# b1 as two rows, a new order of work on all engines, joined y chains and five quantisations on GpSimd in an adaptive-norm FFN kernel

## The chip, the core and the metric

One core of a Trainium2 chip. The metric is device microseconds of one execution. Five engines run their own instruction lists and wait for one another by semaphores: TensorE (PE), VectorE (DVE), ScalarE (ACT), GpSimd (POOL), SyncE (SP, which here only issues DMAs).

## What is computed

x is (2, 1024, 256): two samples of 1024 tokens. Cut to what matters:

```
dg, db, ug, ub = cond @ down_gamma, cond @ down_beta, cond @ up_gamma, cond @ up_beta
down = relu(x @ (down_project * dg + db))               # 256 -> 64, per sample
y    = down @ (up_project * ug + ub) + x                # 64 -> 256
bitlinear(v, w, b) = quant8(rmsnorm(v)) @ ternary(w).T + b
out  = x + bitlinear(gelu(bitlinear(y, w1, b1)), w2, b2)   # 256 -> 1024 -> 256
```

quant8 scales each token by 127 over its largest magnitude, rounds, and divides again. ternary rounds a weight over the mean of all |w| to -1, 0 or 1 and multiplies by that mean. gelu is the exact one.

## The kernel before

The tokens are cut into 8 pairs (k or j, PAIRS) of two slots (s, one for each sample) of 128 tokens. Each engine has its instruction order written out by hand; a helper is called once for each pair or pair and slot, such as `gelu(4, 1)`.

Prologue: `down_weights` and `up_weights` build the conditioned weights (TensorE products, lines 225 to 237, then VectorE, lines 559 to 575). w1 and w2 come by DMA; `absolute_sum` (ScalarE one half, VectorE the other, lines 440 and 577), `weight_sum` (TensorE) and `weight_scale` give the scale, `round_weights`, `lower_weights` and `upper_weights` the ternary weights in fp16. `column_sums` (line 265) adds up w1's columns for the offset that the quantised y carries, `sum_w2` the same for w2.

For each pair: `x_tokens` and `up` (lines 282 to 303) put y for 2 x 128 tokens into PSUM; `largest_y`, `step_y` (VectorE), `square_y`, `quantise_y` (ScalarE, fp16 with an offset). GpSimd's `chain_y(k)` and `inverse_y(k)` (lines 785 to 821) work out the dequantising factor `ydeq` and the inverse with which the bias row is multiplied, nine small instructions for each pair, one waiting for the other; the inverse stands as bf16 pieces beside the quantised y. Pair 0 has `chain_first` instead. `turn_q1(k)` turns this by a DMA transpose on SyncE; pair 0 is turned by TensorE (`transpose_q1`, ScalarE's `copy_q1t`). `first_layer(j, s)` does 4 products of 512 columns with w1 and two with the bias (lines 325 and 333) into PSUM. `gelu(j, s)` writes g, a ring of 4 pairs. `square_g` (line 481, ScalarE) and `largest_g` (line 633, VectorE) read it; `step_g`, then `quantise_g` (line 654) writes fp16 q2. `turn_q2` turns that by DMA for pairs 0 to 5; pairs 6 and 7 go over TensorE (`transpose_q2`) and ScalarE (`copy_q2t`, line 487). `second_layer` (lines 358 and 360), then VectorE's `combine` (line 661) multiplies by `gdeq` (GpSimd's `chain_g`) and adds x, to which GpSimd's `add_b2` (line 852) has added b2. SyncE stores.

b1 is added inside the first layer as bf16 pieces: b1f has nine rows of b1 in each group of 32 partitions, brought by four ScalarE DMAs behind the one of `pk` and behind a memset. GpSimd's `split_b1` (lines 855 to 864) turns them into high, middle and low parts with two passes of a TENSOR_SCALAR and a TENSOR_TENSOR. `keep_warm(n)` is n products of zeros. Nothing else orders the engines than these lists and the semaphores; SyncE's queue is in order too, so a `turn_q2` that waits holds up the turns and stores behind it.

Of the kernel before, what the change touches and what calls it, by code (L numbers as in the profile page):

```python
# [4 lines left out]
P = 128  # L5
SLOTS = 2
# [11 lines left out]
LAST = PAIRS - 1  # L18
ROW = 2 * D + P
# [3 lines left out]
def adaln_ffn(nc, x_tok, x_dim, down_pack, first_pack, w1_t, w2_t, b1_rows, b2_rows, out):  # L23
# [3 lines left out]
    with ExitStack() as ctx:  # L27
# [23 lines left out]
        w2s = sb("w2s", [P, D], F16)  # L51
        b1f = sb("b1f", [P, HALF])
# [16 lines left out]
        neg_half = sb("neg_half", [P, SLOTS])  # L69
# [29 lines left out]
        dpk_in, pk_in, b2_in, b1_zero, b1_in = sem("dpk_in"), sem("pk_in"), sem("b2_in"), sem("b1_zero"), sem("b1_in")  # L99
# [15 lines left out]
        b1_rest, b1_upper, first_done = sem("b1_rest"), sem("b1_upper"), sem("first_done")  # L115
# [9 lines left out]
        q2_ready = sem("q2_ready")  # L125
# [21 lines left out]

        block = ctx.enter_context(nc.Block())

        @block.sync  # L150
        def _(sp):
# [15 lines left out]
            def turn_q1(k):  # L167
                sp.wait_ge(q1_ready, k + 1)
                sp.wait_ge(inv_ready, k + 1)
                sp.dma_start_transpose(q1t[:, k], q1[:, k, :]).then_inc(q1t_in[k - 1], 16)  # L170

            def turn_q2(j, s):
                sp.wait_ge(q2_ready, SLOTS * j + s + 1)
# [20 lines left out]
            turn_q2(1, 0)  # L194
            turn_q2(1, 1)
            turn_q2(2, 0)
            store(0)
            turn_q1(5)
            turn_q2(2, 1)
            turn_q1(6)  # L200
            store(1)
            turn_q2(3, 0)
            turn_q2(3, 1)
            turn_q1(7)
            turn_q2(4, 0)
            turn_q2(4, 1)
            turn_q2(5, 0)
            store(2)
# [10 lines left out]
        def _(pe):  # L219
# [5 lines left out]
            def down_weights():  # L225
# [4 lines left out]
                mm.then_inc(dcond_done, 1)  # L230

# [105 lines left out]
            def transpose_q2(j, s):  # L337

                pe.wait_ge(q2_ready, SLOTS * j + s + 1)
# [44 lines left out]
            first_layer(0, 1)  # L384
            x_tokens(3)
            up(3)
            down(3)
            first_layer(1, 0)
            first_layer(1, 1)
            x_tokens(4)  # L390
            up(4)
            first_layer(2, 0)
            sum_w2()
            first_layer(2, 1)
            x_tokens(5)
            up(5)
            first_layer(3, 0)
            second_layer(0, 0)
            first_layer(3, 1)
            x_tokens(6)  # L400
            up(6)
            first_layer(4, 0)
            second_layer(0, 1)
            second_layer(1, 0)
            first_layer(4, 1)
            x_tokens(7)
            up(7)
            second_layer(1, 1)
            second_layer(2, 0)
            first_layer(5, 0)  # L410
            first_layer(5, 1)
            second_layer(2, 1)
# [3 lines left out]
            first_layer(7, 0)  # L416
            second_layer(3, 1)
            second_layer(4, 0)
            first_layer(7, 1)
            second_layer(4, 1)  # L420
            second_layer(5, 0)
            transpose_q2(6, 0)
            second_layer(5, 1)
            transpose_q2(6, 1)
            transpose_q2(7, 0)
            second_layer(6, 0)
# [6 lines left out]
        def _(a):  # L433
# [38 lines left out]
            def gelu(j, s):  # L472
                a.wait_ge(ffn1_done, SLOTS * j + s + 1)
                if s == 0:
                    a.wait_ge(ydeq_done, j + 1)
# [29 lines left out]
            copy_q1t()  # L505
            round_weights(1)
            square_y(2)
            gelu(0, 0)
            quantise_y(2)
            gelu(0, 1)  # L510
            square_g(0, 0)
            relu(3)
            square_y(3)
            quantise_y(3)
            gelu(1, 0)
            gelu(1, 1)
            square_y(4)
            gelu(2, 0)
            quantise_y(4)
            square_g(0, 1)  # L520
            gelu(2, 1)
            square_y(5)
            quantise_y(5)
            gelu(3, 0)
            square_g(1, 0)
            gelu(3, 1)
            square_g(1, 1)
            square_y(6)
            gelu(4, 0)
            quantise_y(6)  # L530
            square_g(2, 0)
            gelu(4, 1)
            square_g(2, 1)
            square_y(7)
            square_g(3, 0)
            gelu(5, 0)
            quantise_y(7)
            gelu(5, 1)
            square_g(3, 1)
            square_g(4, 0)  # L540
            gelu(6, 0)
            square_g(4, 1)
            square_g(5, 0)
            gelu(6, 1)
# [13 lines left out]
        def _(v):  # L558
# [60 lines left out]

            def largest_y(k):  # L620
# [44 lines left out]
            v.memset(b1f[:], 0.0).then_inc(b1_zero, 1)  # L665
# [6 lines left out]
            down_weights()  # L672
            up_weights()
# [13 lines left out]
            largest_y(2)  # L687
            round_weights(1)
            step_y(2)
            lower_weights(1, 1)  # L690
            add_column_sums()
            upper_weights(1, 1)
            lower_weights(1, 0)
            largest_g(0, 0)
            largest_y(3)
            largest_g(0, 1)
            step_y(3)
# [253 lines left out]
```

## Time and profile before

| | us |
|---|---|
| runs | 75.25, 78.56, 77.22 (median 77.22) |
| the profiled execution | 75.27 |
| its span, first to last instruction | 73.5 |
| mean granted TensorE clock | 0.973 |

The trace's times are of that one execution, counted from the start of its span. "Idle before" names what ended an engine's wait. Start to start of two instructions of one engine is a little less than the duration shown, as the ends overlap.

### The profile page before, as it was taken

Reading aid. Unit: us, or ns where it says so; the run is one execution under the profiler, and the core shown is the slowest. Engines: PE = TensorE matmul, PEld = TensorE weight load, DVE = VectorE, ACT = ScalarE, POOL = GpSimd, SP = SyncE. Lnnn points to the kernel's source line nnn. Section 1 sums busy time; section 2 is a strip of 40 time slices with the busy share of each in tenths; the row PEclk is TensorE's granted clock in tenths of the full one; section 3 lists DMA queues with packets and bytes.
Section 4 is the critical chain, followed back from the end, with each engine's and each line's share of the span. In section 5 each row is a group of like instructions: output and inputs, shape, how many; then the busy total and the mean of one; then the engine's idle time right before and its main releaser. Section 6 shows DMA issues by size and latency. Waiting matters only on the chain.

```text
span 73.5 us, 1375 instructions
## 1 busy us (share of the span) xinstructions
PE 63.8 (87%) x412; PEld 34.9 (47%) x412; DVE 58.1 (79%) x126; ACT 55.1 (75%) x113; POOL 56.5 (77%) x134
## 2 busy tenths in 40 slices
PE   3449995798999999999999999998969998699950
PEld 1042534442733422554355574834416757598830
DVE  4104357998199999799999999999999699999550
ACT  0060157994499949889999999999999999995300
POOL 6700098998889896888879899888899999899700
PEclk9999999955999999999999999999999999999998
DMA  0899999999904004436737709797997996530352
GB/s 6 263 351 288 379 406 430 419 406 428 406 40 92 16 0 89 90 58 123 133 65 143 143 15 270 147 89 167 222 198 145 181 271 118 167 143 16 144 205 73
DMA packets 20478, 13.49 MB, mean 184 GB/s; under 512 B 17748, under 2 KB 18260, under 8 KB 20088
## 3 DMA queue, kind: packets, MB, share of 16 engines
q1 hardware_dynamic: 20256, 12.69, 64.2%
q10 hardware_dynamic: 216, 0.73, 2.9%
q8 instruction: 3, 0.05, 0.3%
q14 instruction: 3, 0.02, 0.1%
HBM read 7.02 MB, written 2.10 MB: 124 GB/s over the span
## 4 chain that ended last, share of the span: by engine, by line
PE 51%; POOL 12%; ACT 11%; DMA 8%; DVE 7%; issue 5%; ACTq 2%; DVEq 0%; POOLq 0%
PE h L325 14%; PE ob L360 12%; DMA b1f<-b_rows 8%; ACT junk_g L481 6%; PE up_ps L302 5%; PE h L333 5%; PE up_ps L293 5%; ACT g L476 5%; POOL b1f L864 3%; DVE q L654 3%; PE ob L252 3%; PE ob L358 2%; POOL b_high L861 2%; PE up_ps L344 2%; ACTq L493 2%
## 5 line engine op out<-in xcount | busy, mean ns | idle before, releaser
L633 DVE TENSOR_REDUCE gtop<-g 128x1 f32<-128x1024 f32 x16 | 19.2, 1207 | 0.7 <-ACT g L476 0.7
L476 ACT ACTIVATE g<-h,ydeq 128x1024 f32<-128x1024 f32 x16 | 17.8, 1127 | 0.2
L481 ACT ACTIVATE junk_g<-g 128x1024 bf16<-128x1024 f32 x16 | 17.1, 1081 | 0.0
L325 PE MATMUL h<-w1q,q1t 128*128 128x512 f16 x64 | 16.5, 380 | 0.0
L360 PE MATMUL ob<-w2q,q2t 128*128 128x256 f16 x128 | 16.3, 272 | 0.0
L360 PEld LDWEIGHTS ob<-w2q,q2t 128*128 128x128 f16 x128 | 12.5, 98 | 1.4
L654 DVE TENSOR_SCALAR q<-g,gm 128x1024 f16<-128x1024 f32 x16 | 11.8, 750 | 0.1
L852 POOL TENSOR_TENSOR x<-x,b 128x512 f32<-128x512 f32 x8 | 10.1, 1271 | 0.0
L325 PEld LDWEIGHTS h<-w1q,q1t 128*128 128x128 f16 x64 | 5.6, 97 | 7.0 <-issue 2.8
L661 DVE SCALAR_TENSOR_TENSOR x<-ob,gdeq,x 128x256 f32<-128x256 f32 x16 | 7.5, 478 | 1.4 <-PE ob L360 1.4
L462 ACT ACTIVATE q<-up_ps,ym 128x256 f16<-128x256 f32 x16 | 6.8, 481 | 0.4 <-DVE ym L629 0.4
L455 ACT ACTIVATE junk_y<-up_ps 128x256 bf16<-128x256 f32 x16 | 6.0, 389 | 1.3 <-DVE ytop L622 1.1
L622 DVE TENSOR_REDUCE ytop<-up_ps 128x2 f32<-128x512 f32 x8 | 5.5, 686 | 1.7 <-PE up_ps L302 1.7
L792 POOL TENSOR_TENSOR yrms<-yvar,neg_half 128x2 f32<-128x2 f32 x7 | 6.1, 873 | 0.6
L358 PE MATMUL ob<-w2s,neg_offset 128*128 128x256 f16 x16 | 4.4, 275 | 2.0 <-DVE x L661 1.7
L861 POOL TENSOR_SCALAR b_high<-b1f,part 128x512 f32<-128x512 bf16 x2 | 1.4, 691 | 5.9 <-DMA b1f<-b_rows 5.8
L830 POOL TENSOR_TENSOR grms<-gvar,neg_half 128x2 f32<-128x2 f32 x7 | 5.5, 780 | 0.6
L302 PE MATMUL up_ps<-wu,act 64*128 64x256 f32 x32 | 5.6, 427 | 0.1
L333 PE MATMUL h<-b1s,q1t 32*128 32x512 bf16 x28 | 5.5, 393 | 0.0
L223 PE MATMUL h<-warm 128*128 128x512 f16 x11 | 4.4, 520 | 1.2 <-DVE warm L664 1.2
L293 PE MATMUL up_ps<-ident,xd 128*128 128x128 f32 x28 | 4.5, 283 | 0.6 <-issue 0.5
L252 PE MATMUL ob<-xd,wd 128*64 128x128 f32 (+2 forms) x24 | 4.6, 513 | 0.0
(104 smaller groups left out, 102.6 us busy)
## 6 DMA issues: line engine op xcount, KB each, us to landing
w<-w_t SPq DMA_DIRECT2D x4, 512.0 KB, 7.7
x<-x_tok SPq DMA_DIRECT2D x2, 1024.0 KB, 13.1
out<-x SPq DMA_DIRECT2D x7, 256.0 KB, 2.3
xd<-x_dim SPq DMA_DIRECT2D x1, 1024.0 KB, 13.0
pk<-first_pack ACTq DMA_DIRECT2D x1, 640.0 KB, 4.2
xd<-x_dim SPq DMA_DIRECT2D x1, 512.0 KB, 9.5
xd<-x_dim SPq DMA_DIRECT2D x1, 256.0 KB, 7.6
out<-x SPq DMA_DIRECT2D x2, 128.0 KB, 1.7
```

The costliest lines, as they stand in the source:

```text
L252: mm = pe.matmul(down_ps[n][H * s:H * (s + 1), :], wd[:, s, c, :], moving, start=(c == 0), stop=(c == DK - 1))
L293: pe.matmul(up_ps[:, s, P * c:P * (c + 1)], x_dims(k)[:, c, s, :], ident32[:, :], start=(c == 0), stop=False, is_transpose=True)
L302: mm = pe.matmul(up_ps[:, s, 0:D], act[rows, k, :], wu[rows, :], start=False, stop=True)
L325: pe.matmul(h_ps[s][:, cols], q1t[:, j, s * DK + c, :], w1q[:, c, cols], start=(i == 0), stop=False)
L333: mm = pe.matmul(h_ps[s][:, HALF * n:HALF * (n + 1)], q1t[rows, j, SLOTS * DK, :].bitcast(BF16), upper_half(bias[rows, :]), start=False, s ...
L360: mm = pe.matmul(out_ps[s], q2t[:, j % RING, s, c, :], w2q[:, c, :], start=False, stop=(c == FK - 1))
L476: a.activation(g[:, j % RING, s, :], h_ps[s][:, :], ACT.Gelu, scale=ydeq[:, j, s:s + 1])\
L481: a.activation(junk_g[:, j % 3, s, :], g[:, j % RING, s, :], ACT.Square, scale=F ** -0.5, accum_out=gmean[:, j, s:s + 1]).then_inc(gsq_don ...
L633: v.tensor_reduce(gtop[:, j, s:s + 1], g[:, j % RING, s, :], AX.X, ALU.max, apply_absolute_value=True)\
L654: v.tensor_scalar(q2[:, j % RING, s, :], g[:, j % RING, s, :], gm[:, j, s:s + 1], OFFSET, ALU.mult, ALU.add).then_inc(q2_ready, 1)
L661: v.scalar_tensor_tensor(x[:, j, s, :], out_ps[s], gdeq[:, j, s:s + 1], x[:, j, s, :], ALU.mult, ALU.add).then_inc(out_ready, 1)
L852: p.tensor_tensor(x[:, j], x[:, j], b2[:, :].unsqueeze(1).broadcast_to([P, SLOTS, D]), ALU.add)\
```

## The change

- b1 comes as one DMA of 2 rows of 512 (ScalarE's queue, no wait); TensorE's `spread_rows` multiplies it by a 2 x 128 pattern of ones, made by GpSimd, so that PSUM has b1's half in nine rows of each group of 32; `split_b1` moves to VectorE, between `down_weights` and `up_weights`, and reads PSUM in its first pass. The memset of b1f goes.
- `pk` is loaded by SyncE right behind `dpk`.
- `keep_warm`: 17 products where there were 11, one fewer ahead of `up_weights`.
- `chain_y` and `inverse_y` run over (0), (1), (2, 3), (4, 5), (6, 7): five chains, not eight. `turn_q1`, and `gelu` of slot 0, wait for the chain that holds their pair.
- `quantise_g` of slot 1 of pairs 1 to 5 is GpSimd's, with a semaphore of its own; `gelu` now also waits, from pair 4 on, for the square and the quantisation of the pair that had its place in the ring.
- The hand-written orders of all engines change: on TensorE `column_sums` ahead of `first_layer(0, 0)`, `weight_sum(1)` after `up(2)`; on VectorE `absolute_sum(1)` after the rounding of w1; on ScalarE the y work ahead of the gelus and `gelu(7, 1)` ahead of `square_g(6, 0)`; SyncE's queue and GpSimd's `add_b2`s are spread anew.

```diff
+CHAINS = [(0, 1), (1, 2), (2, 4), (4, 6), (6, 8)]
+BY_POOL = [(1, 1), (2, 1), (3, 1), (4, 1), (5, 1)]
             sp.dma_start(dpk[:], down_pack).then_inc(dpk_in, 16)
+            sp.dma_start(pk[:], first_pack).then_inc(pk_in, 16)
...
+            def spread_rows():
+                pe.wait_ge(spread_set, 2)
+                pe.wait_ge(b1_in, 16)
+                pe.matmul(ob[:, 0, :], spread_b1[:, :], b1[:, :], start=True, stop=True).then_inc(b1_spread, 1)
...
             down_weights()
-            keep_warm(2)
+            spread_rows()
+            keep_warm(1)
             up_weights()
             down(0)
             x_tokens(0)
+            keep_warm(1)
             up(0)
             keep_warm(3)
             down(1)
+            keep_warm(2)
             weight_sum(0)
+            keep_warm(3)
             x_tokens(1)
             up(1)
             keep_warm(3)
             down(2)
+            keep_warm(1)
             transpose_q1()
             x_tokens(2)
+            up(2)
             weight_sum(1)
-            up(2)
+            column_sums()
             first_layer(0, 0)
-            column_sums()
...
-            a.dma_start(pk[:], first_pack).then_inc(pk_in, 16)
-            a.wait_ge(b1_zero, 1)
-            for r in range(4):
-                a.dma_start(b1f[32 * r + 1:32 * r + 10, :], b1_rows[r % 2]).then_inc(b1_in, 16)
+            a.dma_start(b1[:], b1_rows).then_inc(b1_in, 16)
...
             gelu(7, 0)
             square_g(5, 1)
+            gelu(7, 1)
             square_g(6, 0)
+            copy_q2t(6, 0)
             square_g(6, 1)
+            copy_q2t(6, 1)
             square_g(7, 0)
-            gelu(7, 1)
-            copy_q2t(6, 0)
+            copy_q2t(7, 0)
             square_g(7, 1)
-            copy_q2t(6, 1)
-            copy_q2t(7, 0)
             copy_q2t(7, 1)
...
+            def split_b1():
+                v.wait_ge(b1_spread, 1)
+                v.wait_ge(part_set, 5)
+                for n, rows in enumerate((ob[:, 0, :], b1f[:, :])):
+                    if n:
+                        v.wait_ge(b1_rest, n)
+                    v.tensor_scalar(b1_high[:, :], upper_half(rows), part[:, n:n + 1], 0.0, ALU.mult, ALU.add)\
+                        .then_inc(b1_upper, 1)
+                    v.wait_ge(b1_upper, n + 1)
+                    v.tensor_tensor(b1f[:, :], rows, b1_high[:, :], ALU.add).then_inc(b1_rest, 1)
...
             down_weights()
+            split_b1()
             up_weights()
...
-            absolute_sum(1)
             lower_weights(0, 0)
             upper_weights(0, 0)
+            absolute_sum(1)
+            largest_y(2)
             weight_scale(1)
...
-            def chain_y(k):
-                p.wait_ge(ysq_done, k + 1)
+            def chain_y(n):
+                pairs = slice(*CHAINS[n])
+                p.wait_ge(ysq_done, pairs.stop)
...
+            def quantise_g(j, s):
+                p.wait_ge(gm_ready, j + 1)
+                if j >= RING:
+                    p.wait_ge(q2t_in[j - RING, s], 16)
+                p.tensor_scalar(q2[:, j % RING, s, :], g[:, j % RING, s, :], gm[:, j, s:s + 1], OFFSET,
+                                ALU.mult, ALU.add).then_inc(q2_ready_pool, 1)
...
+            add_b2(0)
+            add_b2(1)
             inverse_y(1)
-            add_b2(0)
             chain_y(2)
             inverse_y(2)
+            add_b2(2)
+            square_scale(1)
+            add_b2(3)
             chain_y(3)
             inverse_y(3)
+            chain_g(0)
+            quantise_g(1, 1)
+            add_b2(4)
+            chain_g(1)
+            quantise_g(2, 1)
+            chain_y(4)
+            inverse_y(4)
+            quantise_g(3, 1)
+            chain_g(2)
+            add_b2(5)
+            quantise_g(4, 1)
+            chain_g(3)
+            quantise_g(5, 1)
```

## Rows read from the trace of the kernel before

**Rows 1.** The page: busy us, share of the span and instructions of each engine
```profile
PE 63.8 (87%) x412; PEld 34.9 (47%) x412; DVE 58.1 (79%) x126; ACT 55.1 (75%) x113; POOL 56.5 (77%) x134
```

**Rows 2.** Busy time by stage; columns: stretch, length, engines' busy us, PEclk, DMA
```profile
18.50:50.00 31.50, 31.43 (x188) 15.68 (x188) 29.09 (x59) 29.00 (x63) 27.06 (x68) 1.00 0.55 111
50.00:64.40 14.40, 12.39 (x90) 7.53 (x90) 13.56 (x25) 14.40 (x25) 13.30 (x25) 1.00 0.85 186
64.40:73.50 9.10, 6.39 (x69) 5.46 (x69) 5.41 (x12) 3.23 (x7) 4.86 (x9) 0.97 0.32 117
```

**Rows 3.** Timeline, prologue: start us, us, engine, line, operation
```profile
4.62 1.23 PE L228 MATMUL h<-dpk 128*128 128x128 f32 x4 [1.99 <-DMA dpk<-down_pack]
...
6.63 1.79 PE L235 MATMUL h<-pk,dpk 128*64 128x512 f32 x4
...
8.92 0.42 DVE L575 TENSOR_TENSOR wu<-wu_gamma,h 128x256 f32<-128x256 f32 x1
...
11.59 0.20 ACT L455 ACTIVATION_READ_ACCUMULATOR junk_y<-up_ps 128x1 f32 x1
...
13.35 0.70 POOL L775 TENSOR_SCALAR yvar<-ymean 128x2 f32<-128x2 f32 x1
...
17.65 0.43 DVE L609 TENSOR_SCALAR w1q<-w1q 128x1024 f16<-128x1024 f16 x1
...
18.24 0.23 POOL L821 TENSOR_TENSOR q<-yrest,q 128x12 bf16<-128x12 f32 x1
...
21.45 1.04 PE L271 MATMUL ob<-w1q,pick 128*128 128x512 f16 x4
```

**Rows 4.** Timeline, from 52 us to the end
```profile
51.99 1.07 ACT L481 ACTIVATE junk_g<-g 128x1024 bf16<-128x1024 f32 x1
...
57.15 2.13 ACT L476 ACTIVATE g<-h,ydeq 128x1024 f32<-128x1024 f32 x2
...
59.14 1.08 ACT L481 ACTIVATE junk_g<-g 128x1024 bf16<-128x1024 f32 x1
...
60.18 1.08 ACT L481 ACTIVATE junk_g<-g 128x1024 bf16<-128x1024 f32 x1
...
63.30 1.13 ACT L476 ACTIVATE g<-h,ydeq 128x1024 f32<-128x1024 f32 x1
...
67.37 0.76 DVE L654 TENSOR_SCALAR q<-g,gm 128x1024 f16<-128x1024 f32 x1
...
68.85 0.60 ACT L487 ACTIVATE q2t<-up_ps 128x512 f32<-128x512 f32 x1 [1.78 <-PE up_ps L344]
...
70.83 0.48 DVE L661 SCALAR_TENSOR_TENSOR x<-ob,gdeq,x 128x256 f32<-128x256 f32 x1 [0.50 <-PE ob L360]
```

**Rows 5.** Groups of instructions (count, busy us, mean ns), and the issues of one transfer
```profile
L633 DVE TENSOR_REDUCE gtop<-g 128x1 f32<-128x1024 f32 x16 | 19.2, 1207 | 0.7 <-ACT g L476 0.7
...
L852 POOL TENSOR_TENSOR x<-x,b 128x512 f32<-128x512 f32 x8 | 10.1, 1271 | 0.0
...
L661 DVE SCALAR_TENSOR_TENSOR x<-ob,gdeq,x 128x256 f32<-128x256 f32 x16 | 7.5, 478 | 1.4 <-PE ob L360 1.4
...
L638 DVE TENSOR_SCALAR gstep<-gtop 128x2 f32<-128x2 f32 x7 | 1.4, 202 | 0.0
...
L861 POOL TENSOR_SCALAR b_high<-b1f,part 128x512 f32<-128x512 bf16 x2 | 1.4, 691 | 5.9 <-DMA b1f<-b_rows 5.8
...
L614 DVE TENSOR_TENSOR b1s<-b1f,ob 128x512 f32<-128x512 f32 x1 | 0.7, 675 | 0.0
...
q2t<-q SPq DMA_TRANSPOSE x12, 3.1
```

**Rows 6.** Busy time and granted clock from 15 to 18 us, columns as above
```profile
15.00:18.00 3.00, 3.00 (x14) 1.12 (x12) 2.93 (x7) 2.22 (x8) 2.68 (x11) 0.50 1.02 413
```

**Rows 7.** Timeline, one meeting of GpSimd and VectorE
```profile
21.65 1.27 POOL L852 TENSOR_TENSOR x<-x,b 128x512 f32<-128x512 f32 x1
...
21.86 1.62 DVE L604 TENSOR_SCALAR w2q<-w 128x1024 f16<-128x1024 f32 x1
```

More of the change, by code:

```diff
@@ L18 @@
 LAST = PAIRS - 1
+CHAINS = [(0, 1), (1, 2), (2, 4), (4, 6), (6, 8)]
+CHAIN_OF = [n for n, (a, b) in enumerate(CHAINS) for k in range(a, b)]
+BY_POOL = [(1, 1), (2, 1), (3, 1), (4, 1), (5, 1)]
+BY_DVE = [(j, s) for j in range(PAIRS) for s in range(SLOTS) if (j, s) not in BY_POOL]
 ROW = 2 * D + P
@@ L694, in _ @@
             largest_g(0, 0)
-            largest_y(3)
+            largest_y(4)
+            step_y(4)
             largest_g(0, 1)
-            step_y(3)
+            copy_w2_sums()
             step_g(0)
             quantise_g(0, 0)
-            upper_weights(1, 0)
+            largest_y(5)
+            step_y(5)
             quantise_g(0, 1)
-            largest_y(4)
             largest_g(1, 0)
-            step_y(4)
             largest_g(1, 1)
+            largest_y(6)
+            step_g(1)
@@ L706, in _ @@
+            step_y(6)
+            quantise_g(1, 0)
             largest_g(2, 0)
-            copy_w2_sums()
-            largest_y(5)
-            step_g(1)
-            step_y(5)
-            quantise_g(1, 0)
+            combine(0, 0)
             largest_g(2, 1)
-            quantise_g(1, 1)
+            largest_y(7)
             step_g(2)
+            step_y(7)
+            combine(0, 1)
+            quantise_g(2, 0)
             largest_g(3, 0)
-            largest_y(6)
-            combine(0, 0)
@@ L718, in _ @@
-            step_y(6)
-            quantise_g(2, 0)
-            combine(0, 1)
             largest_g(3, 1)
-            quantise_g(2, 1)
+            combine(1, 0)
+            step_g(3)
             largest_g(4, 0)
-            combine(1, 0)
-            largest_y(7)
+            quantise_g(3, 0)
             largest_g(4, 1)
-            step_g(3)
+            combine(1, 1)
             step_g(4)
-            combine(1, 1)
-            step_y(7)
-            quantise_g(3, 0)
-            quantise_g(3, 1)
@@ L733, in _ @@
             largest_g(5, 0)
+            combine(2, 0)
+            largest_g(5, 1)
             quantise_g(4, 0)
-            largest_g(5, 1)
-            quantise_g(4, 1)
             step_g(5)
-            combine(2, 0)
+            combine(2, 1)
             quantise_g(5, 0)
-            combine(2, 1)
             largest_g(6, 0)
+            largest_g(6, 1)
             combine(3, 0)
-            largest_g(6, 1)
-            quantise_g(5, 1)
             step_g(6)
             combine(3, 1)
+            quantise_g(6, 0)
@@ L747, in _ @@
             combine(4, 0)
-            quantise_g(6, 0)
+            largest_g(7, 0)
             quantise_g(6, 1)
-            largest_g(7, 0)
             combine(4, 1)
@@ L753, in _ @@
             combine(5, 0)
+            largest_g(7, 1)
             quantise_g(7, 0)
-            largest_g(7, 1)
             combine(5, 1)
@@ L798, in inverse_y @@
-            def inverse_y(k):
-                def spread(a):
-                    return inverse(k).rearrange("p (s n c) -> p s n c", s=SLOTS, n=2)[:, :, :, 1 + a:8 + a:3]
-                def wide(column):
-                    return column.unsqueeze(2).unsqueeze(3).broadcast_to([P, SLOTS, 2, 3])
-                if k == 0:
+                p.wait_ge(yvar_done, n + 1)
+                p.tensor_tensor(yrms[:, pairs, :], yvar[:, pairs, :], neg_half[:, 0:pairs.stop - pairs.start, :], ALU.pow)\
+                    .then_inc(yrms_done, 1)
@@ new lines, in chain_y, with inverse_y, wide @@
+                p.wait_ge(yrms_done, n + 1)
+                p.tensor_tensor(yroot[:, pairs, :], yvar[:, pairs, :], yrms[:, pairs, :], ALU.mult).then_inc(yroot_done, 1)
+                p.wait_ge(ym_ready, pairs.stop)
+                p.tensor_tensor(ydeq[:, pairs, :], yrms[:, pairs, :], ystep[:, pairs, :], ALU.mult).then_inc(ydeq_done, 1)
+            def inverse_y(n):
+                pairs = slice(*CHAINS[n])
+                count = pairs.stop - pairs.start
+                def spread(a):
+                    rows = q1[:, pairs, HALF:ROW].bitcast(BF16)
+                    return rows.rearrange("p k (s n c) -> p k s n c", n=2, c=32)[:, :, :, :, 1 + a:8 + a:3]
+                def wide(columns):
+                    return columns.unsqueeze(3).unsqueeze(4).broadcast_to([P, count, SLOTS, 2, 3])
+                if n == 0:
```

193 lines of the change are left out of this document (90 added, 103 removed).

## The prediction, made before the changed kernel was run

> **What bounds the kernel now.** First the page's busy shares [rows 1]: TensorE 87%, the other three 75 to 79%, so no total is the answer. Then the busy time by stage [rows 2]: from 18.5 to 50 us TensorE is busy for all but 0.1 us; from 50 to 64.4 ScalarE is busy throughout while TensorE has 2 us free; in the last 9.1 us ScalarE has 3.2 us of work and TensorE 6.4: the tail is a chain, not a load.
>
> Then the timeline of the prologue [rows 3]. ScalarE has the squares of the first pair at 11.59 + 0.20 = 11.79, but GpSimd starts its first y chain at 13.35: it has waited 5.9 us for b1's DMAs and then split b1 in 2 x (0.69 + 1.27) = 3.9 us [rows 5]. The chain ends with the inverse at 18.47; VectorE has w1 rounded at 18.08; first_layer(0,0) and column_sums are done at 22.49.
>
> Last the timeline of the tail [rows 4]. The last gelu (pair 7, slot 1) ends at 64.43, since four squares stand ahead of it on ScalarE. Then one after another: VectorE's quantise (7,0), largest (7,1), a combine, a step and quantise (7,1), which ends at 68.13; TensorE's turn; ScalarE's copy, 68.85 to 69.45, after 1.8 us of waiting; second layer and the last combine, which ends at 71.31. The last store takes the rest of the span.
>
> **The change, part by part.**
>
> *b1 as two rows.* GpSimd loses the 3.9 us, and four ScalarE DMAs become one small one. TensorE gets one fp32 product of 512 columns; L235 is two such in 1.79 us [rows 3], so 0.9 each. It stands behind down_weights, which ends at 4.62 + 1.23 = 5.85: b1 is spread at 6.8. VectorE gets four instructions. Below: two TENSOR_SCALARs at half of a quantisation's 0.76 for 1024 columns [rows 4], two TENSOR_TENSORs at L614's 0.68 [rows 5], 2.1. Above: all four at L614's 0.68 and a tenth each between them for the semaphores, 3.0. I take 2.6, the middle, since one of the TENSOR_SCALARs reads PSUM as L614 does: 6.85 to 9.45. Behind it on VectorE waits up_weights, now 8.5 to 9.34; it moves to 9.45 to 10.3, +0.9. up(0) waits for it, then largest_y(0) and every scale. What hides the rest of the 2.6 is VectorE's wait until 8.5 for L235; without that cover the whole 2.6 would show.
>
> *packs on SyncE.* pk and the loads behind it are issued about 0.4 us later than now. TensorE uses pk at 6.63 now, and after the spread and one warm product at about 7.15. Cost nothing; without that cover at most 0.4.
>
> *filling products.* One less before up_weights, seven more behind it. The granted clock is 0.50 from 15 to 18 us [rows 6], that is the 1.2 GHz level. At present this costs nothing, as GpSimd's chain ends later (18.47). If it fell again now, down(2) would cost up to 1 us more; if the products hold it, nothing. I take 0: the products stand where TensorE waits.
>
> *the new prologue.* GpSimd starts its chain with the squares, 11.79 + 0.85 = 12.6, and it ran 5.1 us (13.35 to 18.47): 17.7, or 16.9 if the instructions that were drawn out by VectorE's traffic aren't. w1 is rounded at 18.08 + 0.85 - 1.2 = 17.7, as the absolute sum (a 1024-column reduce, 1.2 [rows 5]) moves behind it. But weight_sum(1) waits for that sum, 18.8, and stands with column_sums (1.0 [rows 3]) ahead of the first layer, which starts at 20.4. With its 1.3 both are done at 21.75, 0.7 us before the present 22.49. The first gelu comes some 0.6 later than now but with quantise_y(2) behind it. After relu(3), for which ScalarE waits either way, I have ScalarE 0.1 to 0.3 ahead.
>
> *y chains joined.* Three chains of nine small GpSimd instructions go, about 3 us each. Pairs 2, 4 and 6 now wait for the squares of 3, 5 and 7. Walking the queues in order with these durations, the inverse of 2 and 3 is there at 28.0, turned by DMA (3.1 us [rows 5]) at 31.1, wanted at 32.2; that of 6 and 7 at 46.7, turned at 49.8, wanted at 50.8. One us of cover each; without it TensorE stalls one for one.
>
> *five slots of g on GpSimd.* VectorE loses 5 x 0.67 = 3.3 us (0.75 less the overlap with the next), against the 2.6 of b1. GpSimd's price has no row. Below: VectorE's own 0.75. Above: 2.5, L852's 1.27 for 512 columns twice. I take 1.4, twice L861's 0.69 for 512 columns [rows 5], the same operation. The Trainium skill (GPSIMD Engine Reference, Elementwise — side-by-side cycle accounting) gives its best case as some 1.8 cycles at 1.2 GHz per element, an estimate of 1.5 us; by it the five would be 0.5 us longer together and the end the same. A slot is later by 0.65 and GpSimd's queue. By the walk (1,1) is done at 39.3 and turned at 42.4, wanted at 45.3; (5,1) at 55.0 and 58.1, wanted at 61.9. Hidden; at 2.5 us still hidden.
>
> *the order in loop and tail.* From 51.99 ScalarE has nine squares at 1.04, four gelus at 1.00 (start to start [rows 4]) and four copies at 0.53: 9.4 + 4.0 + 2.1 = 15.5. Without a wait that ends at 67.5; it ends at 69.45, as the last gelu is late. The new order puts gelu (7,1) four squares from the end, and by my walk gets there 0.5 ahead: 67.05. VectorE, from the step of pair 7 (41.7 in the walk) to quantise (7,1), has ten largest_g at 1.12, eight quantisations at 0.67, eleven combines at 0.40 (means of [rows 5] less 0.08 of overlap) and six steps at 0.29: 11.2 + 5.4 + 4.4 + 1.7 = 22.7, and 1.15 us of waits for others: 65.55 instead of 68.13. From there to the last combine the 71.31 - 68.13 = 3.2 us stay: 68.7. ScalarE's end and VectorE's agree: -2.6 us.
>
> *contention.* A GpSimd instruction that runs holds back VectorE's quick scalar forms: L604 was issued at 21.86 while L852 ran from 21.65 to 22.92, and took 1.62 in all; without its wait it is a 0.7 us instruction [rows 7]. So one meeting costs up to what is left of the GpSimd instruction, 0.9 here. For five quantisations I charge 0.5 us together, between 0 (none meets) and 7 (all do at full length), near the low end, as the eight b2 additions met VectorE so in few places. The Trainium skill (SBUF — State Buffer, Who interferes with whom) says that whichever of the two starts first keeps the shared ports for its whole instruction and the other blocks fully; the trace agrees.
>
> Sum: -2.6 + 0.5 = **-2.1 us**. The profiled execution took 75.27 us (73.5 of span): 73.2, with a span of 71.4. It is near the lowest of the runs shown (75.25); on their median it is 77.22 - 2.1 = **75.1 us**.
>
> **The rivals.** (A) *The port decides.* GpSimd's quantisations fall on VectorE's quick forms in its fullest stretch, and quantise (7,1) slips. For it: VectorE is busy 13.6 of 14.4 us there [rows 2], and both engines quantise once the same gm is ready, so they start together. Against: the additions meet it seldom. The gain is gone from 2.6 us of holding on, three meetings of 0.9; if all five quantisations and two additions meet at 0.9 it is 6.3 - 2.6 = +3.7, if only the five, 4.5 - 2.6 = +1.9, 79.1 us. This is the skill's rule taken at its full length. Chance 0.15.
>
> (B) *The prologue's loss is carried through.* All scales are 0.9 later, weight_sum(1) waits for the moved sum, and b2 additions, now two in a row, hold step_y(2) for up to 1.27: the first gelu starts 1.4 us later than now. For it: TensorE has no slack from 18.5 to 50. Against: work that came behind the first gelu is now ahead of it. Net -2.1 + 1.4 = -0.7: 76.5. Chance 0.27.
>
> (C) *Nothing meets.* No GpSimd instruction holds VectorE, and the waits of the walk (1.15) mostly fall away: -2.6 - 0.7 = -3.3, 73.9. For it: ScalarE's 15.5 us would then be the only bound. Chance 0.2.
>
> **How the numbers follow.** The forecast 0.38, (B) 0.27, (C) 0.2, (A) 0.15. A measurement of this kernel tells about 2%, 1.5 us. Faster by more: nearly all of the forecast's cases and (C), 0.58. Within: (B), the forecast's poor end and the mild half of (A), 0.3. Slower: the rest of (A), 0.12. The likeliest case alone: 74.2 to 76.0. The range goes from (C) on a low execution, 72.9, over (B) to half of (A), 77.9.
>
> **What would show it.** Right: up_weights on VectorE ends near 10.3; GpSimd's first chain starts near 12.6; the first gelu starts at 22.4 to 23.2; the last gelu ends by 61; the last copy by 67.5; GpSimd quantises in 1.4. Wrong: VectorE quantisations or steps drawn out beyond a us beside GpSimd's (A); relu(3) behind 27.5 (B); products that wait for a DMA turn, which would say that the joined chains aren't covered; a granted clock of 0.5 behind 18 us.

## The result, and the profile after

| | kernel before | changed kernel |
|---|---|---|
| median of 11 runs | 77.3 (75.0 to 81.04) | 76.8 (76.31 to 77.33) |
| profiled execution | 75.27 | 76.61 |
| its span | 73.5 | 74.8 |

75.1 us was forecast. The medians lie 0.65% apart, the changed kernel lower. The ratio 1.019 (95% interval 1.013 to 1.025) sets the changed kernel's runs against only the two lowest of before (75.0 and 75.25); the other nine took 77.14 to 81.04, the changed kernel's eleven agree within 1.0 us. So the change made the kernel steadier; that it is faster by 2% is not shown. Profile against profile, it lost 1.3 us where 2.1 were forecast as a gain. The miss is 3.4 us of span (74.8 against 71.4).

First the page of the changed kernel, its busy rows (as [rows 1]), and by stage (as [rows 2]: stretch, length, busy us of PE, PEld, DVE, ACT, POOL, PEclk, DMA share, GB/s; the first stretch starts where the first layer and column_sums are done).

```profile
PE 67.2 (90%) x420; PEld 35.8 (48%) x420; DVE 59.3 (79%) x124; ACT 55.0 (73%) x113; POOL 49.0 (66%) x110
```
```profile
22.20:50.00 27.80, 26.23 (x156) 12.57 (x155) 25.23 (x47) 24.94 (x53) 21.98 (x47) 1.00 0.61 99
50.00:64.40 14.40, 13.76 (x100) 8.34 (x98) 12.75 (x22) 14.06 (x23) 11.44 (x18) 1.00 0.86 185
64.40:74.80 10.40, 6.66 (x69) 5.51 (x69) 6.71 (x15) 5.22 (x10) 4.28 (x10) 1.00 0.28 102
```

The reader is to see two things. TensorE, busy throughout up to 50 us before, now has 1.6 us free there. And the last stretch is 10.4 us long, not 9.1, with VectorE's work in it grown from 5.4 to 6.7. TensorE's waits, as the view of waits sums them (us in total, times, longest), name both:

```profile
PE ob L379 <- DMA q2t<-q: 1.5, 1, 1.5
PE up_ps L365 <- DVE q L691: 1.3, 2, 1.0
...
PE ob L379 <- DVE x L698: 0.5, 1, 0.5
```

The first is one wait in the middle; here is its timeline. second_layer(1, 0) at 43.74 waited for a turn that SyncE had begun to issue at 39.04 and that landed after 4.66 us, where [rows 5] has 3.1. Turns of q1 stand directly ahead of it and behind it.

```profile
37.78 1.20 SPq L184 DMA_TRANSPOSE q1t<-q  x1
...
39.04 1.30 SPq L188 DMA_TRANSPOSE q2t<-q  x1
...
40.43 1.28 SPq L184 DMA_TRANSPOSE q1t<-q  x1
...
41.76 2.16 SPq L188 DMA_TRANSPOSE q2t<-q  x1
...
43.74 0.28 PE L379 MATMUL ob<-w2s,neg_offset 128*128 128x256 f16 x1 [1.46 <-DMA q2t<-q]
...
46.14 1.11 ACT L505 ACTIVATE g<-h,ydeq 128x1024 f32<-128x1024 f32 x1 [1.01 <-PE h L354]
```

The second is in the tail: two of VectorE's quantisations (0.74 us alone) took 1.44 and 1.63 beside GpSimd's additions of b2 (L897), and TensorE's transposition waited 1.0 us for the second.

```profile
60.25 1.28 POOL L897 TENSOR_TENSOR x<-x,b 128x512 f32<-128x512 f32 x1
60.64 1.44 DVE L691 TENSOR_SCALAR q<-g,gm 128x1024 f16<-128x1024 f32 x1
...
61.75 1.12 ACT L505 ACTIVATE g<-h,ydeq 128x1024 f32<-128x1024 f32 x1
...
63.33 1.27 POOL L897 TENSOR_TENSOR x<-x,b 128x512 f32<-128x512 f32 x1
...
63.52 1.63 DVE L691 TENSOR_SCALAR q<-g,gm 128x1024 f16<-128x1024 f32 x1
...
65.20 0.62 PE L365 MATMUL up_ps<-ident,q 128*128 128x128 f16 x8 [1.00 <-DVE q L691]
...
68.70 0.75 DVE L691 TENSOR_SCALAR q<-g,gm 128x1024 f16<-128x1024 f32 x1
...
72.16 0.48 DVE L698 SCALAR_TENSOR_TENSOR x<-ob,gdeq,x 128x256 f32<-128x256 f32 x1 [0.50 <-PE ob L381]
```

The last gelu ends at 62.87 (64.43 before), yet the last quantisation ends at 69.45 (68.13 before): ScalarE's gain was made in part and did not reach the end. And the prologue, where TensorE's products matter:

```profile
3.99 2.07 PE L251 MATMUL ob<-b,spread_b 2*128 2x512 f32 x2
...
6.10 0.75 DVE L652 TENSOR_SCALAR b_high<-ob,part 128x512 f32<-128x512 bf16 x1 [1.12 <-PE ob L251]
...
8.29 1.07 PE L273 MATMUL h<-pk,wd 128*64 128x128 f32 x8
...
9.19 0.42 DVE L601 TENSOR_TENSOR wu<-wu_gamma,h 128x256 f32<-128x256 f32 x1
...
9.29 1.12 PE L314 MATMUL up_ps<-ident,pk 128*128 128x128 f32 x4
...
10.20 0.63 PE L238 MATMUL h<-warm 128*128 128x512 f16 x1
...
10.76 0.76 PE L323 MATMUL up_ps<-wu,act 64*128 64x256 f32 x4
```

VectorE is done with up_weights at 9.61, but up(0) starts at 10.76 (9.49 before): TensorE itself is late. Its eight L273 products take 1.07 us (421 ns each); in the kernel before the same eight, L252 there, take 0.60 (272 ns each), from 8.25:

```profile
8.25 0.60 PE L252 MATMUL h<-pk,wd 128*64 128x128 f32 x8
...
9.49 0.70 PE L302 MATMUL up_ps<-wu,act 64*128 64x256 f32 x4
```

### The profile page after: what moved, and what is told of

It is laid out like the page before. It is cut to its first block, busy times and chain, and to the rows that moved or that the text cites. A ratio compares the mean times of both kernels' runs of the same rounds, so it can differ in the third digit from the quotient of the medians.

```text
span 74.8 us, 1372 instructions
## 1 busy us (share of the span) xinstructions
PE 67.2 (90%) x420; PEld 35.8 (48%) x420; DVE 59.3 (79%) x124; ACT 55.0 (73%) x113; POOL 49.0 (66%) x110
## 4 chain that ended last, share of the span: by engine, by line
PE 49%; ACT 12%; DVE 10%; DMA 9%; issue 9%; POOL 6%; SPq 2%; DVEq 0%; ACTq 0%; POOLq 0%
PE h L346 7%; ACT junk_g L510 7%; DMA q2t<-q 6%; PE h L238 5%; PE up_ps L323 5%; PE ob L381 5%; PE ob L273 5%; PE up_ps L314 4%; DVE q L691 4%; ACT g L505 3%; DVE gtop L670 3%; DMA dpk<-down_pack 3%; PE ob L251 3%; PE h L354 3%; PE h L256 3%
## 5 line engine op out<-in xcount | busy, mean ns | idle before, releaser
L691 DVE TENSOR_SCALAR q<-g,gm 128x1024 f16<-128x1024 f32 x11 | 10.5, 955 | 0.1
L897 POOL TENSOR_TENSOR x<-x,b 128x512 f32<-128x512 f32 x8 | 10.2, 1275 | 0.1
L238 PE MATMUL h<-warm 128*128 128x512 f16 x17 | 6.1, 453 | 1.2 <-DVE warm L701 1.2
L868 POOL TENSOR_TENSOR grms<-gvar,neg_half 128x2 f32<-128x2 f32 x7 | 6.2, 890 | 0.6
L889 POOL TENSOR_SCALAR q<-g,gm 128x1024 f16<-128x1024 f32 x5 | 6.0, 1202 | 0.5
L323 PE MATMUL up_ps<-wu,act 64*128 64x256 f32 x32 | 5.7, 432 | 0.1
L865 POOL TENSOR_SCALAR gvar<-gmean,iw,ew 128x2 f32<-128x2 f32 x7 | 2.6, 371 | 3.5 <-ACT junk_g L510 3.5
## 6 DMA issues: line engine op xcount, KB each, us to landing
xd<-x_dim SPq DMA_DIRECT2D x1, 1024.0 KB, 12.6
```

The costliest lines, as they stand in the source:

```text
L238: pe.matmul(h1[:, HALF:HALF + columns], warm[:, 0:P], warm[:, 0:columns], start=True, stop=True)
L323: mm = pe.matmul(up_ps[:, s, 0:D], act[rows, k, :], wu[rows, :], start=False, stop=True)
L691: v.tensor_scalar(q2[:, j % RING, s, :], g[:, j % RING, s, :], gm[:, j, s:s + 1], OFFSET, ALU.mult, ALU.add).then_inc(q2_ready, 1)
L897: p.tensor_tensor(x[:, j], x[:, j], b2[:, :].unsqueeze(1).broadcast_to([P, SLOTS, D]), ALU.add)\
```

## The experiments

Medians in us. The kernel before was timed beside each group of runs: medians 77.63 (a1 to a4), 78.36 (b1, c1, c2, c4), 77.2 (d1 to d3, e1) and 77.18 (f1 to f3).

| run | median | span profiled | VectorE's quantise, mean ns | TensorE's largest wait behind 22 us | first gelu starts | from there to the last combine's start |
|---|---|---|---|---|---|---|
| the changed kernel | 76.8 | 74.8 | 955 | turn 1.5 | 23.05 | 49.1 |
| a2_no_b2_late | 74.97 | 72.7 | 811 | turn 1.4 | 22.64 | 47.4 |
| a3_turn_later | 75.55 | 73.3 | 1002 | turn 1.7 | 22.28 | 48.4 |
| b1_b2_moved | 75.94 | 74.5 | 861 | turn 1.8 | 23.54 | 48.3 |
| d1_store_late | 75.9 | 73.3 | 1001 | quantise 1.0 | 22.83 | 47.9 |
| d2_store_b2 | 74.35 | 72.7 | 860 | 0.4 | 23.09 | 46.9 |
| d3_less_warm | 73.85 | 72.2 | 862 | 0.4 | 22.59 | 46.9 |

The last two columns are needed since the medians mix two things. The first six rows have the same prologue, yet their first gelu starts between 22.28 and 23.54 us. What an edit behind the prologue is worth shows better from the first gelu on: two executions of one kernel, d3 and f3, agree there to 0.01 us, and the kernel before has 49.04 and 49.23 (a1).

### Is it the port?

**a2_no_b2_late.** The additions of b2 to pairs 6 and 7 cover one column only (the rest of that work is left out).

```diff
+                n = D if j < 6 else 1
+                p.tensor_tensor(x[:, j, :, 0:n], x[:, j, :, 0:n], b2[:, 0:n].unsqueeze(1).broadcast_to([P, SLOTS, n]),
...
```

> The changed kernel, with b2 added to one column of 256 for pairs 6 and 7, so the rest of b2 is left out there; same instructions and order. Port theory: the quantisations of g on VectorE that took 1.44 and 1.63 us beside the additions of pairs 6 and 7 take 0.75; end about 1.5 us earlier, 75.3. Rival (the tail is set by the gelus that are already late, or by the turns): at most 0.4 us.

74.97, 1.8 less. The two quantisations are back at 0.74:

```profile
59.74 0.19 POOL L898 TENSOR_TENSOR x<-x,b 128x2 f32<-128x2 f32 x1
```
```profile
60.15 0.74 DVE L691 TENSOR_SCALAR q<-g,gm 128x1024 f16<-128x1024 f32 x1
...
62.33 0.74 DVE L691 TENSOR_SCALAR q<-g,gm 128x1024 f16<-128x1024 f32 x1
```

They give back 0.70 + 0.89 = 1.6 us, and from the first gelu on the kernel is 1.7 us shorter; up(0) also started 0.3 us earlier in that execution. The meetings with two additions cost about 1.6 us of the 3.4.

**c4_all_on_dve.** All sixteen quantisations of g on VectorE; each of slot 1 stands in its list right behind the one of slot 0.

```diff
-BY_POOL = [(1, 1), (2, 1), (3, 1), (4, 1), (5, 1)]
+BY_POOL = []
...
```

> The changed kernel with all of g quantised by VectorE, slot 1 right behind slot 0; GpSimd's five go. The prediction's step: VectorE gains 3.3 us by the move and all of it is wanted, so undoing it costs 1 to 3 us (78 to 79.5). Rival: VectorE waits anyhow and the turns come earlier (0.75 instead of 1.12 us and no wait for GpSimd): within 0.5 us of 76.8, or earlier.

76.86: no difference (49.4 from the first gelu on, against 49.1). In this kernel GpSimd's five do no harm, and VectorE's relief of 3.3 us does next to no good.

### Is it the turn?

**a3_turn_later.** The turn of q2(1, 1) goes ahead of the one of q1(5).

```diff
+            turn_q2(1, 1)
             turn_q1(5)
-            turn_q2(1, 1)
```

> The changed kernel, with the DMA turn of q1 of pair 5 issued behind that of q2 (1,1) and not ahead of it. Turn theory: q2 (1,0) took 4.66 us to land since turns issued close together share something; with the q1 turn away it lands in 3.1 to 3.8 and TensorE's 1.46 us wait ahead of second_layer(1,0) falls to under 0.7; end 0.7 to 1.0 us earlier. Rival (the turn of q2 (1,1) takes the place of the one moved, or the wait is given back later): within 0.3 us.

75.55, ratio to before 0.978 (0.970 to 0.986). The wait ahead of second_layer(1, 0) is gone; another of 1.7 us, for the turn of q2(5, 1), has come at 62.4. The median fell by 1.25 us, but not all of it is the exchange: from the first gelu on it is worth 0.7 us (49.1 to 48.4), and in the profiled execution the first gelu also came 0.77 us earlier, out of a prologue whose code is the same.

**b1_b2_moved.** From a3: GpSimd's additions one place earlier each, so that none stands in VectorE's tail.

```diff
             add_b2(3)
+            add_b2(4)
...
-            add_b2(4)
+            add_b2(5)
...
-            add_b2(5)
+            add_b2(6)
...
             quantise_g(5, 1)
+            add_b2(7)
             chain_g(4)
-            add_b2(6)
             chain_g(5)
-            add_b2(7)
```

> The kernel of a3_turn_later with GpSimd's additions of b2 for pairs 4 to 7 each one place earlier, so that those of pairs 6 and 7 no longer run beside VectorE's quantisations of (6, 0) and (6, 1). Computes the reference. Port theory: those two quantisations take 0.75, not 1.43 and 1.60; end 0.7 to 1.5 us earlier than a3_turn_later's 75.55: 74.0 to 74.9. Turn theory: in a3_turn_later TensorE waited 1.69 us for the turn of q2 (5, 1) in the tail, which takes the place of the port: at most 0.4 us earlier.

75.94: nothing gained on a3 (0.1 us from the first gelu on), though the quantise's mean fell from 1002 to 861 ns; TensorE still waits 1.8 us for the turn.

**d1_store_late.** From a3: store(2) behind the last three turns of q2.

```diff
-            store(2)
             turn_q2(4, 1)
...
             turn_q2(5, 1)
+            store(2)
```

> a3_turn_later with the store of pair 2 behind the turns of (4, 1), (5, 0) and (5, 1) and not ahead of them. In a3_turn_later the store waited until 55.57 for its combine, with the turn of (4, 1) ready at 53.4 behind it, and TensorE waited 1.69 us for the turn of (5, 1). Queue theory: the turns are issued some 0.6 us earlier and that wait falls to about 1.0; end 0.5 to 0.7 earlier than a3_turn_later (75.55): 75.0. Rival (turns that follow one another land more slowly, and VectorE's held quantisations set the end): within 0.2 us.

75.9: the turn's wait is gone, and TensorE waits 1.0 us for VectorE's quantise instead. The median gained nothing on a3; from the first gelu on it gained 0.5 us, which the later first gelu (22.83 against 22.28) hides in the span.

**d2_store_b2.** The edits of b1 and d1 at once, on a3.

> d1_store_late and b1_b2_moved together. If the port and the turn hid each other, each alone giving little over a3_turn_later, both together give 1.0 to 1.5 us: 74.2 to 74.6. If the turns alone bound the tail: as d1_store_late.

74.35. Against a3's median each edit alone gave +0.4 us and both together -1.2; from the first gelu on they gave 0.1, 0.5 and 1.5 us. So two waits lay in the same stretch, and the removal of one let the other show: the turn's 1.8 us in b1, the quantise's 1.0 us in d1, and in d2 no wait above 0.4 us.

### The prologue and the filling products

**a4_warm_as_before.** The changed kernel with the filling products of the kernel before (3, 2, 3, 3).

```diff
             down(1)
-            keep_warm(2)
             weight_sum(0)
-            keep_warm(3)
             x_tokens(1)
```

> The changed kernel with the filling products as in the kernel before: 3, 2, 3, 3. If they hold the clock: 0.50 is granted for some us in the prologue again and the times spread as those of the kernel before do (75 and 77); the best no lower than now or 0.5 us lower. If they only cost time: the first gelu comes 0.4 to 0.8 us earlier, the granted clock stays 1.00 and the end is 0.4 to 0.8 us earlier.

76.77, equal in the median. But of ten executions seven were at 76.2 to 77.0 with a granted clock of 1.00, three at 78.3 to 79.0 with 0.974 to 0.978; the changed kernel's eleven are all at 1.00. The products seem to buy that; three executions of ten are few, and a2, which has the products, has one of four at 0.975. In the median they cost nothing.

**c1_before_warm.** The kernel before with six filling products at the same places.

> The kernel before with six of the filling products of the change and nothing else (two and three ahead and behind weight_sum(0), one behind down(2)). Clock theory: every run is granted 0.99 or more, where runs of the kernel before lie between 0.955 and 1.00, and none is above 78; median 0.3 to 1 us below the kernel before. Rival (products only cost time): the spread stays, and the median rises by 0.3 us or more.

77.43, all four at a granted clock of 1.00: no gain, so the clock is not what makes this kernel take 77. Its profile shows a late turn of q1(5) (it landed after 4.2 us, in the kernel before after 2.6; TensorE waits 0.9, ScalarE 1.1) and then an addition of b2 that meets a quantisation:

```profile
60.16 1.28 POOL L855 TENSOR_TENSOR x<-x,b 128x512 f32<-128x512 f32 x1
```
```profile
60.30 1.70 DVE L657 TENSOR_SCALAR q<-g,gm 128x1024 f16<-128x1024 f32 x1
```

The additions are a hazard of the kernel before too; in its profiled execution of 75.27 they happen to miss VectorE's quantisations of g. From the first gelu on this execution takes 51.35 us against 49.04, about the distance between 75 and 77.

**c2_b1_only.** The kernel before with the part on b1 alone (two rows, spread_rows, split_b1 on VectorE), nothing else.

> The kernel before with b1's part of the change alone: two rows by one DMA, spread by TensorE, split by VectorE between down_weights and up_weights. The prediction had up_weights end 0.9 us later and GpSimd's first chain start 0.7 earlier, net a gain of up to 0.7 at the first layer. What the changed kernel's trace shows: VectorE's up_weights ends only 0.3 later, but TensorE's products run at half rate until about 11 us instead of about 8, and up(0) starts 1.2 us later. If the spread causes that, first gelu and end come 0 to 0.5 us later than in the kernel before; if VectorE's split does, up(0) starts when up_weights ends.

75.66 (75.45 to 75.91, all at 1.00). up(0) starts at 11.59, 2.1 us later than before; yet no execution at 77. GpSimd, free of 3.9 us, waits 10.2 us for the first squares. Of the 2.1 us, 0.5 came through: the first gelu starts at 22.29 (21.79 before), and from there on both take 49.04 us.

**d3_less_warm.** From d2, without the product between spread_rows and up_weights and the one ahead of up(0).

```diff
             spread_rows()
-            keep_warm(1)
             up_weights()
...
             x_tokens(0)
-            keep_warm(1)
             up(0)
```

> d2_store_b2 without the filling product ahead of up_weights and the one ahead of up(0). Each takes 0.5 to 0.6 us at half rate. If they stand on the path: 0.5 to 1.0 us earlier. If TensorE's rate rises later without them: no gain or a wider spread of the times, and a granted clock below 1.00 in some runs.

73.85. up(0) starts at 9.85, not 10.88. The first gelu comes 0.5 us earlier than in d2, and the rest is the same. This is the fastest version; it differs from the changed kernel in orders and in two filling products only.

### The order of the tail

**e1_tail_order.** c2_b1_only with only the change's orders of the tail: on ScalarE gelu(7, 1) ahead of square_g(6, 0), with TensorE's and VectorE's lists to match.

```diff
             square_g(5, 1)
-            square_g(6, 0)
-            square_g(6, 1)
-            square_g(7, 0)
             gelu(7, 1)
+            square_g(6, 0)
             copy_q2t(6, 0)
-            square_g(7, 1)
+            square_g(6, 1)
...
```

> c2_b1_only (75.66) with the change's order of the tail alone: ScalarE's gelu (7, 1) ahead of square (6, 0) and the copies one place earlier, TensorE's first_layer(7, 1) ahead of second_layer(3, 1) and its turns one place earlier, VectorE's largest (7, 1) ahead of quantise (7, 0). The prediction's step: ScalarE's last copy ends 1.9 us earlier, the kernel about 1.9: 73.8. Rival (VectorE's list in the tail sets the end, not gelu (7, 1)): 0 to 0.7 us.

78.16, 2.5 us slower than c2, but this is not the price of the order alone. Up to 46.5 us the two profiled executions run the same to 0.1 us. Then a turn takes 1.88 us to issue, in c2 1.30, and the turn of q1(5) ahead of it lands after 4.2 us, not 2.6. TensorE waits for it:

```profile
46.51 1.30 SPq L177 DMA_TRANSPOSE q2t<-q  x1
```
```profile
46.61 1.88 SPq L177 DMA_TRANSPOSE q2t<-q  x1
...
49.49 1.04 PE L334 MATMUL h<-w1q,q1t 128*128 128x512 f16 x4 [0.88 <-DMA q1t<-q]
```

This is the late turn of c1, and it stands ahead of everything that e1 moves. By gelu(5, 0) e1 has lost 1.1 us. Behind it ScalarE waits for TensorE ahead of its copies, 3.3 us in all (the view of waits; 2.7 in c1), and additions of b2 meet VectorE's quantisations at 61.08, as in c1, and at 70.00:

```profile
ACT q2t L497 <- PE up_ps L353: 3.3, 3, 2.2
```
```profile
61.08 1.69 DVE L673 TENSOR_SCALAR q<-g,gm 128x1024 f16<-128x1024 f32 x1
...
70.00 1.40 DVE L673 TENSOR_SCALAR q<-g,gm 128x1024 f16<-128x1024 f32 x1
```

From the first gelu on e1 takes 51.73 us, c2 49.04 and c1 51.35, and c1 has the late turn without the new order. So the order by itself brought none of the 1.9 us that the prediction's step gives it here; held against c1 it cost some 0.4 us. Why all four executions of e1 take 77.4 us or more and all four of c2 less than 76 stays open, as the code is the same until then.

### What is the kernel before to be held against?

**a1_before_again.** The kernel before, unchanged, as one of the kernels tested.

> The kernel before, unchanged, as a second profile and a spread. Its eleven times lie at 75.0 to 75.3 (two) and 77.1 to 78.6 and above (nine); the changed kernel's eleven lie within 76.3 to 77.3. Theory P: the two groups of the kernel before differ in the clock that TensorE is granted in the prologue, where its row showed 0.50 for 3 us: a profiled execution of about 77 us shows 0.50 for longer than 3 us, or behind 20 us where TensorE has no slack, and a lower mean clock than 0.973. Rival Q: they differ by DMA: the same clock, but loads or turns that land later. Ratio 1.00 either way.

75.11, 78.4, 77.02, 75.87, with granted clocks of 1.00, 0.955, 0.996 and 0.974. 77.02 us came at 0.996 and 75.87 at 0.974: the clock doesn't divide them.

**f1_before_store.** The kernel before with store(0) behind turn_q1(5) and turn_q2(2, 1).

> The kernel before with one edit: store(0) is issued behind turn_q1(5) and turn_q2(2, 1) instead of ahead of them. Theory S (the executions of the kernel before that take about 77 us are those in which the turn of q1(5) comes late behind the store, as in the profile of the run with filling products, where TensorE waited 0.9 us for it and the additions of b2 then met VectorE's quantisations): with the turn ahead of the store, most executions lie at 75.0 to 75.8 and the median falls by 1.2 us or more. Rival (the store has no part in it; the late executions come from how the prologue's rate falls out, and the order of stores and turns is neutral): the executions stay spread over 75 to 80 with a median within 0.6 us of the kernel before. Profiled execution: by theory S gelu of (5, 0) starts within 0.3 us of where it starts in the 75.25 us execution, and mean time of VectorE's quantisations of g is 0.74 to 0.77 us; by the rival one of the two is off (0.80 us or more) in any execution at 77.

76.31 (75.04 to 78.42, 12 runs) against 77.18; ratio 0.994 (0.986 to 1.002). This lies between what the two expected. Seven of twelve stay above 76. The order of store and turns is at most a part of it.

### GpSimd's share once more

**f2_d3_all_on_dve.** d3 with all quantisations of g on VectorE, by the same edit as in c4; **f3_d3_again**: d3 unchanged.

> The fastest version so far (turns ahead of the stores, b2's additions moved, no filling products in the middle of the prologue) with all quantisations of g on VectorE, none on GpSimd. Theory G (in this version VectorE is nearer its bound, since its stalls beside b2 and the turns are gone, so the five quantisations that GpSimd took, 0.75 us of VectorE each, count in part): slower than the fastest version of 73.85 us by 0.5 to 1.5 us, that is 74.4 to 75.4. Rival N (the quantisation step is hidden here as in the changed kernel, where the same edit gave 76.86 against 76.8): 73.6 to 74.2.

> The fastest version again, unchanged, timed more often, for its interval and beside the two others of this call: 73.4 to 74.3 us, 3 to 5% below the kernel before's median of about 77.2 and 1 to 2.5% below its best executions of 75.0 to 75.2. If the 73.85 us were the luck of four executions, the median lies above 74.6.

f2 76.59 (75.9 to 77.69), f3 74.05 (73.69 to 74.81; ratio to before 0.976, 0.968 to 0.984). The five quantisations, worth nothing in the changed kernel, are worth 2.5 us here (2.6 from the first gelu on), more than either theory said. From 50 to 64 us, f2 and then f3 (columns as above), and between them f2's largest wait on TensorE:

```profile
50.00:64.00 14.00, 11.24 (x78) 6.85 (x79) 13.90 (x24) 11.71 (x19) 7.10 (x13) 1.00 0.79 177
```
```profile
PE ob L379 <- DVE x L696: 3.1, 2, 1.9
```
```profile
50.00:64.00 14.00, 13.23 (x102) 7.99 (x100) 13.16 (x23) 13.64 (x23) 10.32 (x16) 1.00 1.02 197
```

In f2 VectorE is full (13.90 of 14) and TensorE has nearly 2.8 us free, waiting for combines that stand behind the quantisations. In f3 the work is shared and TensorE and ScalarE run on.

## Why the prediction was wrong, point by point

**The step that failed** is the one on the order in loop and tail, -2.6 us, and in it the sum of VectorE's list. From the step of pair 7 to the end of quantise (7, 1) it gave VectorE 22.7 us of work and 1.15 of waits, from 41.7 to 65.55. The changed kernel does the instructions that were counted, but takes 27.3 us for them (42.13 to 69.45) and is 3.9 us late at the end. VectorE stood idle 2.6 us in that stretch, not 1.15: 0.74 and 0.70 for gelus, 0.85 for TensorE. Two quantisations took 1.6 us more than their 0.74 beside additions of b2. The late start is 0.4 us, and the rest of the work came out 0.5 longer than summed. From there to the last combine the 3.2 us stayed, as forecast. The step took ScalarE's list and VectorE's list, each without most of the other's waits, and held both to be met because the two sums agreed. The last gelu did come earlier (it ended at 62.87 against 64.43, where "by 61" was forecast), and the term counted on VectorE following it.

The runs divide the miss of 3.4 us. Turns, store and additions put in other places give 2.2 (49.1 to 46.9 from the first gelu on, d2). Two filling products less give 0.5 in the prologue (d3). The rest, 0.8 us (a span of 72.2 against 71.4), stays open. The walk described a kernel with hardly a wait or a meeting. The nearest to it is d3, at 73.85 and 74.05 (f3) against the 73.2 of the sum; three changes of order and two filling products lie between it and the changed kernel.

**Contention** was charged with 0.5 us, and for the wrong instructions. None of the five quantisations on GpSimd held a VectorE instruction in the changed kernel's profile by more than 0.1 us; once it went the other way, GpSimd's at 48.62 taking 1.53 us beside a VectorE quantisation that had begun at 48.42. What met VectorE's quantisations were additions of b2, three times, 0.71, 0.70 and 0.89 us longer: 2.3 us held, some 1.6 of it on the path (a2). In other versions one of the five does meet: in a3, b1, d1 to d3 and f3 a quantisation of VectorE takes 1.33 or 1.34 us beside GpSimd's of (4, 1). That "the eight b2 additions met VectorE so in few places" was read off one execution, and c1 shows that the order of the kernel before can have such meetings too. Rival (A), with a chance of 0.15, had the mechanism and two additions in its price; its own place, the five quantisations, was wrong for this kernel. By the Trainium skill (SBUF — State Buffer, Who interferes with whom) the one that starts first keeps the port and the other blocks; these rows agree in both directions.

**The turns.** "One us of cover each" used 3.1 us for a turn, the middle of twelve. The joined chains were covered, as forecast. But a turn issued between two others landed after 4.66 us, and TensorE waited 1.46 us; the exchange in a3 gives back 0.7 from the first gelu on. The step took a transfer's price from a median and not from its place in the queue. "Products that wait for a DMA turn" stood among the signs, but as a sign that the joined chains weren't covered. They were: the turn that came late was one of q2, which hangs on no y chain.

**The prologue.** The spread took 2.07 us, not 0.9, from a wrong reading of L235. Its two products of four instructions did take 1.79 us together, but each instruction took 0.87 to 1.12: the two products, one for each half of the array's columns, ran side by side. L256, the same two in the changed kernel, takes 1.98 for both; the spread, alone, took two such instructions one after the other:

```profile
L235 PE MATMUL h<-pk,dpk x4: 874/996/1116, 6.6 to 7.5; 128*64 128x512 f32 x4
```
```profile
L251 PE MATMUL ob<-b,spread_b x2: 1056/1136/1217, 4.0 to 5.0; 2*128 2x512 f32 x2
```

In c2 the products behind the spread start 1.6 us later than before (8.24 against 6.63) and up(0) 2.1 us. The changed kernel loses only 1.3 there, for a reason that the prediction put at nothing: with `pk` behind it on SyncE, `dpk` landed 2.1 us after its issue, with `pk` on ScalarE's queue after 3.9 (3.8 in c2), so that the first product started at 2.84 and not at 4.62. The splitting in 2.6 us was right, and up_weights ended at 9.61 (10.3 forecast). What then held up(0) was TensorE's rate, on which the prediction has nothing. GpSimd's chain started at 13.23 (12.6), the first layer was done at 22.24 (21.75), the first gelu began at 23.05 (22.4 to 23.2). That is 1.26 us later than before, near the 1.4 of rival (B); but relu(3) came at 26.68, 0.2 us ahead of the kernel before as forecast, and not behind 27.5 as (B) has it. That the median, 76.8, lies next to (B)'s 76.5 is luck. "Filling products, 0" held for the median, the clock never fell to 0.50, and all executions agreed; that two of them held up(0) by 1.0 us, and the first gelu by 0.5, was missed (d3).

**GpSimd's share.** Quantising took it 1.12 us, not 1.4, and less than the 1.5 us estimated by the page of the Trainium skill (GPSIMD Engine Reference, Elementwise — side-by-side cycle accounting). VectorE's relief of 3.3 us was set against b1's 2.6 as if it were all on the path; in this kernel it was worth nothing (c4), in the fastest version 2.5 us (f2).

**The base.** The sum was made on an execution of 75.27 and carried to the median of 77.22. c1 shows that a 77 can be another course of events with waits of its own, not the same course made longer, so a difference can't be moved from the one to the other. The courses part at two DMAs: in c1 and e1 store(0) and the turn of q1(5) behind it both landed after 4.2 us, in the profiles of the kernel before (both near 75), and of c2, after 2.5 and 2.6. That the 77s of the kernel before are this course is likely, as the distance fits, but none of them was profiled. Why it falls one way or the other stays open: neither clock (c1, a1) nor the store's place (f1) settles it. The range, too, has a slip: its low end, (C) on a low execution, is 75.25 - 3.3 = 72.0, not 72.9.

## What to carry to other kernels

When two engines' lists both come out as long as the forecast, look for what couples them: transfers, shared ports and buffers to be freed, each priced at the place where it will stand and not by its group's mean. After a change of many orders, look in the new trace for the few waits that are left and remove them together: two waits in one stretch hide each other (on a3, b1's or d1's edit alone 0.1 and 0.5 us; both 1.5), and a relief that measures as zero may be worth 2.5 us behind them. Before a single edit is priced, look where its execution parts from the one that it is held against: a loss that arises ahead of the edit (e1, 1.1 us) isn't the edit's.

## What the runs showed of the hardware

- TensorE's products ran at about half rate at the start and changed to full rate at times that differ between executions of the same code: the eight L273 products behind `pk` took 1.07 us in the changed kernel, 0.99 in a3, whose code is the same there. The L323 product of up(0) took 0.76 in the changed kernel, 0.70 in a3 and 1.17 in b1. The granted clock shows 1.00 all the while. The Trainium skill (TensorE: Matmul & The Clock Gate, Part 1: The HAM clock gate) says that the number of slow products at the start varies from run to run of one kernel; the rows agree. With it up(0) starts anywhere from 10.08 (a3) to 10.88 us (d2).
- Issuing a turn took SyncE 1.2 to 1.3 us, but 2.16 when others were under way. In the changed kernel landing took 2.6 us for a q1 (the median; the longest 4.0) and 3.6 for a q2 (the longest 5.1).
- The same turn at the same time of the same list landed after 2.6 us in one execution and after 4.2 in another (c2 and e1).
- A load of 129 KB landed 2.1 to 2.2 us after its issue in all eleven profiles in which the next load, of 640 KB, came behind it in the same queue, and 3.8 to 4.2 us in all six in which that load was issued at the same time from ScalarE's queue.
- GpSimd's scalar form on 1024 columns, fp32 to fp16: 1.12 us, and 1.53 when VectorE had begun first.
